# Attention queries projected transposed, moved by DMA, and three buffers of queries, keys and values

## The reference

```
n = layernorm(x + relu(x @ W1[lang] + b1) @ W2[lang] + b2) * gamma[lang] + beta[lang]
q = n @ Wq.T  (16 heads of 16);  k = n @ Wk.T;  v = n @ Wv.T   (one head of 16 for all)
x = x + softmax(causal(q k / 4)) v @ Wf.T + bf
h = gelu(x @ fc1.T + b);  y = [h @ fc2.T, h @ experts[idx].T] + b
x = x + ffn(y)            (gated 256 -> 1024, two 1024 x 1024 layers, 1024 -> 256)
```

## Time and profile before

| | |
|---|---|
| median of 3 runs | 1158.77 us (1157.55 to 1159.96) |
| profiled execution | 1157.74 us, its span 1156.0 us |
| granted TensorE clock, mean | 0.995 of full speed |
| busy: PE | 1117.5 us (97%) |
| busy: PEld / DVE / ACT / POOL | 892.6 / 804.4 / 594.7 / 214.6 us |
| chain that ended last | PE 89%, DVE 6% |

### The profile page before, as it was taken

One profiled execution on the slowest core, in us unless ns is written; L12 is line 12 of the kernel. 1 busy time (PEld: TensorE's weight loads), 2 busy tenths in 40 slices (PEclk: granted clock), 3 DMA queues, 4 the chain that ended last, 5 costly groups with the idle time before them and its releaser, 6 DMA issues.

```text
span 1156.0 us, 18793 instructions
## 1 busy us (share of the span) xinstructions
PE 1117.5 (97%) x6148; PEld 892.6 (77%) x6178; DVE 804.4 (70%) x1440; ACT 594.7 (51%) x989; POOL 214.6 (19%) x266
## 2 busy tenths in 40 slices
PE   4899999999998999999999999999999999999998
PEld 3567777777775788888888888888888888888886
DVE  2877777776776557756577875778656887568875
ACT  1355655555555634533365654556445565455653
POOL 2233333343345444452000000000000000000000
PEclk9999999999999999999999999999999999999999
DMA  4342122122143456654515443044440444304420
GB/s 122 111 149 60 53 59 63 48 60 63 47 160 124 151 187 202 227 188 150 204 35 164 140 167 115 10 164 146 162 137 0 163 146 163 137 8 145 145 91 37
DMA packets 66765, 135.97 MB, mean 118 GB/s; under 512 B 13793, under 2 KB 28017, under 8 KB 66545
## 3 DMA queue, kind: packets, MB, share of 16 engines
q1 hardware_dynamic: 57696, 114.49, 30.5%
q10 hardware_dynamic: 9024, 20.97, 5.0%
HBM read 107.65 MB, written 30.41 MB: 119 GB/s over the span
## 4 chain that ended last, share of the span: by engine, by line
PE 89%; DVE 6%; SPq 2%; issue 1%; DMA 1%; ACT 1%; POOL 0%; DVEq 0%; POOLq 0%; ACTq 0%
PE bank L1531 35%; PE bank L1493 10%; PE bank L1319 7%; PE bank L1543 5%; PE bank L1469 4%; PE bank L1463 4%; PE bank L1253 4%; PE bank L1234 3%; DVE neg_max L891 2%; PE bank L1274 2%; PE bank L1311 2%; PE bank L1216 2%; PE bank L1200 2%; PE bank L1237 1%; PE bank L1189 1%
## 5 line engine op out<-in xcount | busy, mean ns | idle before, releaser
L1531 PE MATMUL bank<-op_lo,w_ring 128*128 128x512 f32 x896 | 348.6, 389 | 0.0
L1531 PE MATMUL bank<-op_hi,w_ring 128*128 128x512 f32 x896 | 348.6, 389 | 0.0
L1066 DVE TENSOR_TENSOR op_lo<-x_blk,op_hi 128x512 fp32r<-128x512 f32 x288 | 193.8, 684 | 30.4 <-ACT op_hi L764 30.3
L764 ACT ACTIVATE op_hi<-x_blk 128x512 fp32r<-128x512 f32 x288 | 162.8, 620 | 73.6 <-PE bank L1531 69.3
L1531 PEld LDWEIGHTS bank<-op_lo,w_ring 128*128 128x128 f32 x896 | 168.2, 188 | 34.9
L1531 PEld LDWEIGHTS bank<-op_hi,w_ring 128*128 128x128 f32 x896 | 168.2, 188 | 34.9
L891 DVE TENSOR_REDUCE neg_max<-bank 128x2 f32<-128x512 f32 (+1 forms) x192 | 126.0, 685 | 48.0 <-remote 39.7
L617 ACT ACTIVATE p<-bank 128x512 f32<-128x512 f32 x192 | 111.3, 599 | 71.9 <-PE bank L1253 68.2
L788 ACT ACTIVATE x_blk<-x_blk,scales 128x512 f32<-128x512 f32 x96 | 69.3, 722 | 67.0 <-DVE x_blk L1119 28.9
L1493 PE MATMUL bank<-tile_hi,ffn_w 128*128 128x512 f32 x256 | 101.5, 396 | 0.0
L1493 PE MATMUL bank<-tile_lo,ffn_w 128*128 128x512 f32 x256 | 101.5, 396 | 0.0
(11 more groups left out here) (124 smaller groups left out, 1850.0 us busy)
## 6 DMA issues: line engine op xcount, KB each, us to landing
w_ring<-hid_scratch SPq DMA_DIRECT2D x112, 512.0 KB, 4.6
hid_scratch<-comb ACTq DMA_DIRECT2D x8, 1792.0 KB, 7.6
comb<-in_hid_d ACTq DMA_DIRECT2D x6, 768.0 KB, 5.1
xt<-in_x_t SPq DMA_DIRECT2D x16, 256.0 KB
xtok<-in_x_tok SPq DMA_DIRECT2D x16, 256.0 KB
resid<-in_x_t SPq DMA_DIRECT2D x16, 256.0 KB, 3.1
x_scratch<-x SPq DMA_DIRECT2D x16, 256.0 KB, 2.6
tile_in<-x_scratch SPq DMA_DIRECT2D x8, 512.0 KB, 4.1
```

Of the source, the lines that this page charges most:

```text
L764: nc.scalar.activation(op_hi[:, o % OP_RING, k], x_blk[:, operand_home(o), k], ACT.Copy).then_inc(s["op_hi"], 1)
L1066: nc.vector.tensor_tensor(op_lo[:, o % OP_RING, k], x_blk[:, operand_home(o), k], op_hi[:, o % OP_RING, k].bitcast(F32), ALU.subtract).the ...
L1531: last = mm(banks[first_bank + m][:, :], w, read(v[:, q % OP_RING, k, :]), start=k == 0 and v is op_hi and i not in (P2, P3), stop=k == KB ...
```

## The change

- Queries are projected transposed: four matmuls of 256 columns give both halves of the heads, with the weights' columns reordered. ACT writes the high part (`queries_high`), DVE the rest (`queries_low`), and SP moves both by six DMAs into the rows of `q_t` (`move_queries`). The 16 transposes, ACT's four copies and POOL's two copies are gone.
- Values are projected in free columns of the key projection. ACT copies the result to `kv` and writes `keys` from it with scale and bias (`keys_high`); DVE takes the rests (`keys_low`); PE transposes `kv` (`values_transposed`) and DVE copies the values (`values_of`). POOL no longer touches keys or values.
- `q_t`, `keys` and `values` have three buffers each, and the loop has three iterations in its body.
- The order on each engine is new, and some waits with it.
- The store of the first chunk of combined weights is issued by ACT after the last maxima have been moved (`store_chunk` in iteration 15), not at the end of iteration 14.

SP's list, and the new DMAs:

```diff
+            def move_queries(n, slot):
+                sp.wait_ge(s["q_low"], n + 1)
+                settle(sp, "sp_settled")
+                for i, part in enumerate((q_high, q_rest, q_high)):
+                    for par in range(2):
+                        row = SLOT * par + HD * i
+                        sp.dma_start(q_t[slot][row:row + HD, :, :].bitcast(F32), part[:, par, :].bitcast(F32)).then_inc(s["q_moved"], 16)
...
-                    load_front(b + 3)
-                    store_x1(b - 1)
+                    load_front(b + 3)
+                    move_queries(b + 2, (step + 2) % SLOTS)
+                    store_x1(b - 1)
                     load_resid(b)
-                    move_maxima(b + 1, 1 - step % 2)
+                    move_maxima(b + 1, (step + 1) % SLOTS)
```

ACT, with the new functions:

```diff
+            def queries_high(n):
+                act.wait_ge(s["q_mm"], n + 1)
+                if not is_first(n):
+                    act.wait_ge(s["q_moved"], 96 * n)
+                nc.scalar.activation(q_high[:, :, :], ring[0][:, :].rearrange("p (a t) -> p a t", a=2), ACT.Copy, scale=QSCALE).then_inc(s["q_hi"], 1)
+            def keys_high(n, slot):
+                act.wait_ge(s["kv_mm"], n + 1)
+                nc.scalar.activation(kv[:, :], ring[1][:, 0:T], ACT.Copy).then_inc(s["kv_out"], 1)
+                act.wait_ge(s["kv_out"], n + 1)
+                for par in range(2):
+                    nc.scalar.activation(keys[slot][:, par, :], kv[:, :], ACT.Identity,
+                                         bias=key_row[:, 2 * par:2 * par + 1], scale=key_row[:, 2 * par + 1:2 * par + 2]).then_inc(s["keys_hi"], 1)
```

DVE's list:

```diff
                 if maxima:
-                    for u in range(6, 10):
+                    for u in range(6, 8):
                         maximum(b + 1, u)
                 if front:
-                    keys_of(b + 2)
+                    queries_low(b + 2)
+                if maxima:
+                    for u in range(8, 10):
+                        maximum(b + 1, u)
+                if front:
+                    keys_low(b + 2, (slot + 2) % SLOTS)
                 if maxima:
                     maximum(b + 1, 10)
                     maximum(b + 1, 11)
                     split_maxima(b + 1)
                 if front:
-                    queries_of(b + 2, 0)
+                    values_of(b + 2, (slot + 2) % SLOTS)
                 if tail:
                     add_residual(b - 1)
-                if front:
-                    queries_of(b + 2, 1)
```

The other new functions, cut:

```diff
+            def keys_low(n, slot):
+                dve.wait_ge(s["keys_hi"], 2 * (n + 1))
+                for par, rows in enumerate((slice(32, 64), slice(96, 128))):
+                    nc.vector.tensor_tensor(keys[slot][rows, par, :], kv[rows, :], keys[slot][rows, par, :].bitcast(F32),
+                                            ALU.subtract).then_inc(s["keys_out"], 1)
+            def queries_low(n):
+                dve.wait_ge(s["q_hi"], n + 1)
+                nc.vector.scalar_tensor_tensor(out=q_rest[:, :, :], in0=ring[0][:, :].rearrange("p (a t) -> p a t", a=2), scalar=QSCALE,
+                                               in1=q_high[:, :, :].bitcast(F32), op0=ALU.mult, op1=ALU.subtract).then_inc(s["q_low"], 1)
+            def values_of(n, slot):
+                dve.wait_ge(s["v_t_mm"], n + 1)
...
+                    nc.vector.tensor_copy(values[slot][:, :, at:at + rows], src[:, :, row:row + rows]).then_inc(s["values_out"], 1)
...
+            def project_queries(n, tail):
+                pe.wait_ge(s["norm_t_out"], n + 1)
...
+                for m in range(KD):
+                    for k in range(KD):
+                        last = mm(ring[0][:, m * T:(m + 1) * T], wq[:, k, m * P:(m + 1) * P], norm_t[:, k, :], start=k == 0, stop=k == KD - 1)
+            def values_transposed(n):
+                pe.wait_ge(s["kv_out"], n + 1)
+                for t in range(NT):
+                    last = nc.tensor.transpose(ring[1][:, T + t * P:T + (t + 1) * P], kv[:, t * P:(t + 1) * P], ident[:, :])
...
+                if softmax and not maxima:
+                    act.wait_ge(s["maxima_moved"], 64 * B)
+                    store_chunk(0)
```

And the waits that changed with it on PE, beside the renamed ones:

```diff
             def adapter_in(n, tail):
-                    pe.wait_ge(s["keys_out"], n)
+                    pe.wait_ge(s["norm_t_out"], n)
                     if tail:
                         pe.wait_ge(s["x1_out"], HEAD + KD * (n - 3))
...
             def max_scores(n, slot, u):
-                if first % 4 == 0:
-                    pe.wait_ge(s["q_t_out"], 4 * n + 2 * t + first // 4 + 1)
                 if u == 0:
-                    pe.wait_ge(s["keys_moved"], 2 * (n + 1))
-                    pe.wait_ge(s["qv_out"], NT * (n + 1))
+                    pe.wait_ge(s["q_moved"], 96 * (n + 1))
+                    pe.wait_ge(s["keys_out"], 2 * (n + 1))
+                    if not is_first(n):
+                        pe.wait_ge(s["max_out"], UNITS * n)
```

407 lines of the change are left out of this document (178 added, 229 removed).

## The result

| | before | after |
|---|---|---|
| median | 1159.37 us | 1223.36 us (1221.30 to 1225.88) |
| ratio | | 1.055, 95% interval 1.053 to 1.058 |
| profiled execution | 1157.74 us, span 1156.0 | 1222.84 us, span 1221.0 |
| granted clock, mean | 0.995 | 0.978 |

The change is slower by 5.5%. The prediction had the sign and named the stalls, but it said +33 us where the span grew by 65.0. I first cut this sum into stages, by the moment at which SP starts to issue the maxima. These rows of SP's timeline end iterations 0, 13 and 14 of the new kernel and answer to the earlier trace rows.

The account below looks back on a forecast made before the run. PE bounds the kernel unless it waits; 1.6 us PE work saved against about 5 us of waits gave a 24.5 us period. Loop +34, head +4, end -5 made +33: 1191 us, own range 1178 to 1204, wider 1166 to 1208.

Parts of the forecast that it names:

- the sum: Whole kernel: loop +34, head +4, iterations 14 and 15 together -5, in all +33 us.
- The rival that named the clock: Loop: PE's clock falls with PE busy 80% of the period; at 0.9, +17 us, 1208 us; chance 0.08.
- Work removed from PE: PE per sample: 3.58 us removed, 1.99 added, net 1.6 less; busy time becomes 19.6 us.
- The first rival: Loop: PE stays the bound and the change pays; period 19.6 to 20.0, 1131 us; chance 0.09.
- Walk, start: Iteration start: products follow adapter_in, so DVE's first maximum comes 5.24 us after it, DVE idle until then.
- Walk, DVE up to the norm: DVE finishes the norm at 13.05; PE is there at about 10.7 and stalls 2.4 us.
- POOL's and ACT's edits cost nothing: Loop: edits on POOL and ACT add 0 to the period; ACT has slack, POOL only loses work.
- Walk, the end: Iteration end: 2.3 us of DVE work up to the residual, for which adapter_in waits; period 24.5 us.
- The moves in the loop: Six query DMAs land at 25 to 26, needed at 28.9: cost nothing, 2.8 us slack.
- The head: First queries pass ACT, DVE and SP, landing at 31.7, DVE's first maximum at 32.5: +4 us, ends 1 and 7.
- The end: Iterations 14 and 15 together: 14 takes 17.6 us instead of 19.0, late store -4; total -5, ends -1 and -7.

Follow-up runs that it names:

- mask2_late: Against the changed kernel, POOL's third mask is held back until the norm is made; 1202.2 us.
- warm_loop: Against the changed kernel, ten extra matmuls with unused results on PE ahead of its wait for the norm, iterations 1 to 13; 1211.5 us.
- loop_order: Changed kernel reordered: third mask held back, norm's transposes later, early products before adapter_in, first max scores right behind it, maxima moved before the x1 store; 1209.2 us.
- qmove_short: Against the changed kernel, only the first two of the six query moves are issued, so scores lack terms; 1219.0 us.
- warm_head: Against the changed kernel, 24 extra matmuls with unused results on PE ahead of its wait for the first queries, iteration -1 only; 1222.6 us.
- loop_head: Against loop_order, the whole front of sample 1 goes ahead of sample 0's maxima in iteration -1, on PE, ACT and DVE; 1209.9 us.

## Why the prediction was wrong

The sign was right; the size was off by half. Two steps failed. In the loop, the sum held TensorE's clock at full speed through a stall of 2.4 us in every iteration, and its falls cost 12 of the 20 us that were missing. In the head, the sum let iterations -1 and 0 run on as before once the first queries had landed, and they lost 8.5 us more; why is open in part. The rival that named the clock came, at 0.08. (The sum itself is 1191.8 and stands as 1191.)

- **Work removed from PE: right.** 19.66 us busy where nothing stalls (19.6 forecast). The first rival, PE as the bound, was wrong for this order; with another order and two of the six moves it is nearly right, but at 21.1 us, not 19.8, so it gives 7 us in the loop and not 27, and that kernel leaves out part of the work.
- **Walk, start: right.** 5.43 us for 5.24.
- **Walk, DVE up to the norm: short by 0.6.** DVE had the norm at 13.6 instead of 13.05, and PE reached it at 11.3 instead of 10.7, since it first waits 0.94 at m4. Both were 0.6 late, so the stall came out at 2.4 all the same. I took 3.10 for the last piece from a row in which no mask lay beside `normalise`. The new order puts it under mask 2. The walk had placed exponentials for POOL's `rstd` only and never asked which POOL instruction runs beside which DVE instruction. mask2_late shows the 0.62 us. "POOL's and ACT's edits cost nothing" is the sentence that failed.
- **Walk, the end: right.** The waits of 0.77 for the maxima and 0.56 for the residual are the forecast's 2.3 us of DVE work. The full-clock period came to 24.9 instead of 24.5, which is 5 of the +20 (13 times 0.4); the mask's 0.62 us is more than all of it.
- **The clock: the step that cost most in the loop.** It was a rival at 0.08 with +17, and it came: the eight intervals with a fall are 1.3 to 2.3 us over 24.9, 13.6 us in sum, and warm_loop gets 12 back. I argued from PE's mean busy share in the iteration (80%). The runs show that the mean does not tell: PE is busy 81% of an iteration in the new kernel (20.23 of 24.93 us) and 83% in mask2_late (20.19 of 24.32), and the clock fell behind seven of 12 stalls of 2.4 us in the one and behind no stall of 1.80 in the other. The length of the stall does not tell by itself either. What else decides stays open. These rows of PE's timeline in loop_order are a stall with the clock at 1.00 behind it (250.45 to 260.00) and a shorter one with the clock at 0.50 behind it (273.71 to 280.54):

```profile
250.45 0.96 PE L1224 MATMUL bank<-keys,q_t 128*128 128x256 f32 x4 [2.24 <-DMA q_t<-q_high]
```

```profile
273.38 1.41 PE L1224 MATMUL bank<-keys,q_t 128*128 128x256 f32 x4 [1.70 <-DMA q_t<-q_high]
```

- **The moves in the loop: right for the wrong number.** They are hidden in this order (qmove_short), but land after 3.4 to 5.3 us where my bounds were 1.94 and 3.1. The last of them lands at 182.9 (177.6 and 5.3) and the next m0 starts at 184.54, so the slack was 1.6 us and not 2.8. The rows for the bounds were small moves and loads that go out alone; no row showed six in a row into 16 partitions. The prediction had cited the Trainium skill ("SBUF — State Buffer", Door 1: The DMA port swizzle) for an estimate of 1.2 us of transfer for a move. It took this once, though the six follow one another: six times 1.2 are 7.2 us, an estimate. The trace agrees with that size: the six land some 1.0 us apart, also where two neighbours in the row write partitions 64 apart, and the last is there 8.2 to 8.8 us after the first issue.
- **The head: the step that cost most of all for its size.** +15.1 for +4. The first issue came where I had placed it (25.20), the landing at 33.9 instead of 31.7, and DVE started 6.6 us late where the forecast has 3.8. Then I let iterations -1 and 0 run on as before, and they lost 4.6 and 3.9 us more. Iteration -1 has nothing that could fill a wait: m4 waits 1.33 us for a maximum, the norm costs 1.43, `maxima_T` 2.19, and the clock is 0.73 for 20 us. qmove_short gives back 5.6 of the 11.2 us of iteration -1 and 3.5 of the 15.1; warm_head gave back nothing clear. The rest was not taken apart, and loop_head, which tried to by order, gained nothing.
- **The end: right by luck.** -4.4 for -5, but iteration 14 gained nothing (+0.3 where -1.4 was forecast), and what follows it gained 4.7 where 4 was.

## What to carry to other kernels

When an order is walked through, walk POOL beside DVE too, not only each engine against PE. When the walk leaves a stall on PE in every iteration, give the time at the lower clock behind it a price of its own: here stalls of 1.7 to 2.4 us were often followed by 3.4 to 6.8 us at 1.2 GHz, and stalls of 1.8 in another order by none. Moves by DMA that are issued in a row land one behind the other: here six took twice as long as two (8.6 against 4.3 us), not the time of one. Give them the place with the most slack, and look for them first in the head, where there is none.

## What the hardware showed that I had not expected

- Some DVE instructions that work from SBUF alone stand until a POOL instruction is over that started before them: 0.73 to 1.35 us (`normalise`, 128x256 twice) and 0.19 to 1.05 (the split's subtraction of two SBUF operands, 128x32), beside a mask of 1.09. Others do not: the statistics, which read `u` in SBUF, kept their 0.75 us beside the mask at 161.05 (160.78 to 161.53), and maxima, which read a bank, their 0.68 to 0.69 in every kernel. The Trainium skill ("GPSIMD Engine Reference", Specifications) names contention on the SBUF interfaces shared with VectorE, for VectorE instructions in a 2-port mode or with two SBUF inputs. The traces agree for the split's, which has two, and show the price, up to the length of the POOL instruction; in which mode `normalise` runs no trace shows. It also goes the other way: in these rows of DVE's and POOL's timelines of the new kernel `keys_low` started first, and the mask, which takes 0.64 at 161.05 and 171.49, took 0.75:

```profile
175.78 0.87 DVE L867 TENSOR_TENSOR keys<-kv,keys 32x256 fp32r<-32x256 f32 x2 [0.40 <-ACT keys L599]
```

```profile
176.39 0.75 POOL L508 TENSOR_SCALAR_AFFINE_SELECT p<-p 128x512 f32<-128x512 f32 x1 [4.26 <-ACT p L607]
```

- PE's granted clock after a stall: 2.42 us at the norm is followed by 0.50 for 3.4 us (167.80 to 171.21), 2.23 us at m0 in loop_order by 0.50 for 6.8 (178.14 to 184.97). Behind a stall of 1.72 in the same kernel it stayed at 1.00 (203 to 212), and so it did behind one of 2.24 (250.45 to 260.00).
- Six SBUF-to-SBUF moves of 128 KB take 8.2 to 8.8 us from the first issue, by one queue or two; two take 4.3 (25.30 to 29.62 in qmove_short).
